# Counting the uncertain rows of a sparsemax on TensorE, with the flags of eight heads in one word

## The reference

```python
def sparsemax(x):                      # last axis: 722 scores
    x = x - jnp.max(x, axis=-1, keepdims=True)
    zs = -jnp.sort(-x, axis=-1)
    cssv = jnp.cumsum(zs, axis=-1) - 1.0
    support = zs > cssv / rho          # rho = 1, 2, ..., 722
    k = jnp.maximum(jnp.sum(support, axis=-1, keepdims=True), 1)
    tau = jnp.take_along_axis(cssv, k - 1, axis=-1) / k
    return jnp.clip(x - tau, 0.0)
scores = jnp.einsum('bhqd,bhkd->bhqk', qh, kh) * scale
out = jnp.einsum('bhqk,bhkd->bhqd', sparsemax(scores), vh)
```

## Time and profile before

| | |
|---|---|
| median of the three runs | 724.58 us |
| time of the profiled execution | 725.45 us |
| its span, first to last instruction | 723.7 us |
| PE busy | 584.8 us (81%) |
| DVE busy | 609.3 us (84%) |
| ACT, POOL busy | 380.7 us (53%), 187.1 us (26%) |
| mean granted TensorE clock | 0.902 of 2.4 GHz |

### The profile page before, as it was taken

The page is one execution under the profiler, slowest core; times in us unless marked ns, Lnnn a source line. Parts: engine busy times, 40 slices in busy tenths (PEclk is TensorE's granted clock), DMA queues, the critical chain, the costliest instruction groups (busy, mean ns, idle before and its releaser), DMA issues.

```text
span 723.7 us, 14347 instructions
## 1 busy us (share of the span) xinstructions
PE 584.8 (81%) x4560; PEld 332.5 (46%) x4560; DVE 609.3 (84%) x2964; ACT 380.7 (53%) x657; POOL 187.1 (26%) x239
## 2 busy tenths in 40 slices
PE   3785989798814998899899998990889988997575
PEld 1343545454402654565455544550445544655242
DVE  5699799977966999999999999994899999999600
ACT  3664565766611755666566646560456665563321
POOL 2511403241220240415033502351014430301301
PEclk9879978999965999999999999996899999996857
DMA  9752131202220113130303030303102111200000
GB/s 315 237 166 72 27 103 47 59 0 71 68 76 0 28 28 101 33 84 15 110 26 95 6 105 28 106 1 84 42 1 78 39 45 31 59 17 14 11 1 11
DMA packets 33471, 44.23 MB, mean 61 GB/s; under 512 B 8353, under 2 KB 26785, under 8 KB 33382
## 3 DMA queue, kind: packets, MB, share of 16 engines
q1 hardware_dynamic: 32332, 41.16, 20.0%
q10 hardware_dynamic: 1056, 2.10, 0.8%
HBM read 23.77 MB, written 1.64 MB: 35 GB/s over the span
## 4 chain that ended last, share of the span: by engine, by line
PE 64%; issue 16%; ACT 11%; DVE 4%; SPq 3%; DMA 1%; POOL 1%; POOLq 0%; DVEq 0%
PE ring L456 33%; PE ring L522 8%; PE ring L545 5%; PE ring L599 5%; PE mix_bank L570 5%; PE ring L495 4%; PE ring L507 3%; ACT qst L674 2%; ACT S L674 2%; SPq L248 2%; ACT ctx L674 1%; DMA S<-in_L_xattn_Wk 1%; SPq L252 1%; ACT v L674 1%; ACT ks L682 1%
## 5 line engine op out<-in xcount | busy, mean ns | idle before, releaser
L929 DVE MAX8 cand<-S 100x8 f32<-100x45 f32 (+1 forms) x2048 | 223.1, 188 | 0.5 <-issue 0.4
L456 PE MATMUL ring<-wv,ctx 128*121 128x512 f16 x576 | 156.7, 392 | 0.0
L456 PE MATMUL ring<-ctx,wk 128*128 128x361 f16 x768 | 136.1, 339 | 4.5 <-DVE ctx L1108 4.5
L798 ACT ACTIVATE pT<-ring 121x800 f32<-121x800 f32 x96 | 80.5, 839 | 75.2 <-PE ring L599 75.2
L674 ACT ACTIVATE S<-ring 100x722 f32<-100x722 f32 x128 | 95.2, 774 | 27.6 <-PE ring L545 27.2
L456 PEld LDWEIGHTS ring<-ctx,wk 128*128 128x128 f16 x768 | 78.9, 104 | 58.6 <-issue 14.9
L333 POOL TENSOR_TENSOR ctx<-ctx_f,ctx 128x484 f16<-128x484 f32 x42 | 50.6, 1205 | 163.8 <-ACT ctx L674 163.4
L545 PE MATMUL ring<-kst,qst 96*100 96x361 f16 x256 | 68.0, 361 | 29.4 <-ACT S L674 12.9
L456 PEld LDWEIGHTS ring<-wv,ctx 128*121 128x121 f16 x576 | 71.8, 137 | 33.4 <-issue 7.9
L599 PEld LDWEIGHTS ring<-qst,kst 99*121 99x121 f16 x768 | 61.5, 150 | 45.5 <-issue 21.7
L341 POOL TENSOR_TENSOR ks<-k_f,ks 128x361 f16<-128x361 f32 x64 | 57.2, 894 | 90.9 <-ACT k_f L686 88.2
(11 more groups left out here) (126 smaller groups left out, 727.3 us busy)
## 6 DMA issues: line engine op xcount, KB each, us to landing
kst<-ks SPq DMA_DIRECT2D x384, 45.1 KB, 1.9
ctx_f<-in_ctx SPq DMA_DIRECT2D x45, 242.0 KB, 2.9
xq<-in_x SPq DMA_DIRECT2D x8, 200.0 KB
xr<-in_x SPq DMA_DIRECT2D x8, 200.0 KB
out_y<-att SPq DMA_DIRECT2D x8, 200.0 KB
S<-in_L_xattn_Wk ACTq DMA_DIRECT2D x1, 1024.0 KB, 6.8
wq<-in_L_xattn_Wq ACTq DMA_DIRECT2D x1, 1024.0 KB, 11.3
wcos<-in_L_ffn_theta SPq DMA_DIRECT2D x1, 1024.0 KB, 10.4
```

The source lines that it names most:

```text
L456: last = nc.tensor.matmul(psum, lhs(c, i), w(c, j), start=(c == 0 and n == 0), stop=(c == DC - 1 and n == 2))
L798: nc.scalar.activation(pT[0:CK, u % 3, :, :], src, ACT.Relu).then_inc(two_read, 1)
L929: last = nc.vector.max(cand[:, h, 8 * n:8 * n + 8], S[0:L, HH * (i % 2) + h, cuts[n]:cuts[n + 1]])
```

## The change

Four things change.

1. The last Newton step takes its step at zero or more, and is written apart.
2. The test on DVE is one comparison: all eight ranks at or over tau, written as bf16 marks laid out by rank (`by_rank`: 8 ranks x 8 heads x 16 pieces; the comparison runs through `cand` in its own order, so successive marks go to places 128 marks apart). The first MAX8 of the next half waits for it.
3. PE does the sum: one product of `n_over`, then one of 128 columns for each rank, with minus ones for ranks 0 to 6 and ones for rank 7. It leaves 16 + 1 numbers a head in one PSUM row. `sum_flags(i)` moves from phase i + 1 to the end of phase i, right behind the scores of half i + 1 and ahead of `o_of` and the next keys.
4. `read_flags` sums the 17 numbers, multiplies each flag by 2^h, and sums them to one word. `settle` loads that word once, and tests fours, twos and ones of its bits by register arithmetic. Heads are refined from the lowest number up.

```diff
             def sum_flags(i):
                 pe.wait_ge(flag_ready, i + 1)
                 if i > 0:
                     pe.wait_ge(aT_ready, 2 * i)
-                nc.tensor.matmul(flag_ps, ones[:, :], n_over[:, :], start=True, stop=False)
-                nc.tensor.matmul(flag_ps, minus[:, :], n_now[:, :], start=False, stop=True).then_inc(flag_sum, 1)
+                nc.tensor.matmul(flag_ps[:, :, PIECES], ones[:, :], n_over[:, :], start=True, stop=True)
+                for r in range(8):
+                    last = nc.tensor.matmul(flag_ps[:, :, 0:PIECES], (one_b if r == 7 else minus_b)[:, :],
+                                            by_rank[:, r, :, :], start=(r == 0), stop=(r == 7))
+                last.then_inc(flag_sum, 1)
...
             def maxes(i, h):
                 dve.wait_ge(two_read, seen2(("s", i, h)))
+                if h == 0 and i > 0:
+                    dve.wait_ge(flag_ready, i)
...
-                    last = nc.vector.scalar_tensor_tensor(t, step_t[:, :], STRETCH[turn], t, ALU.mult, ALU.add)
...
+                nc.vector.scalar_tensor_tensor(t, step_t[:, :], 0.0, t, ALU.max, ALU.add).then_inc(tau_ready, 1)
                 dve.wait_ge(tau_ready, i + 1)
-                marks = over[:, :, :].rearrange("p g (n r) -> p g n r", r=8)
-                counted(nc.vector.tensor_tensor(marks[:, :, :, 7:8], pieces[:, :, :, 7:8],
-                                                t4.broadcast_to([L, HH, PIECES, 1]), ALU.is_lt))
-                n = counted(nc.vector.tensor_tensor(marks[:, :, :, 0:7], pieces[:, :, :, 0:7],
-                                                    t4.broadcast_to([L, HH, PIECES, 7]), ALU.is_ge))
-                n = counted(nc.vector.tensor_tensor(fold[:, :, 2:2 + NCAND // 2], over[:, :, 0:NCAND // 2],
-                                                    over[:, :, NCAND // 2:NCAND], ALU.add))
-                n = counted(nc.vector.reduce_sum(n_now[:, :], fold[:, :, :], AX))
-                nc.vector.scalar_tensor_tensor(n_now[:, :], n_now[:, :], -float(PIECES), n_over[:, :],
-                                               ALU.add, ALU.min).then_inc(flag_ready, 1)
+                nc.vector.tensor_tensor(by_rank.rearrange("p r g n -> p g n r"), pieces, t4.broadcast_to([L, HH, PIECES, 8]), ALU.is_ge).then_inc(flag_ready, 1)
...
+            def read_flags(i):
                 dve.sem_clear(check_step)
                 dve.wait_ge(flag_sum, i + 1)
-                nc.vector.scalar_tensor_tensor(code[:, :], flag_ps, 0.5, order_c[:, :],
+                nc.vector.reduce_sum(lost[:, :], flag_ps, AX).then_inc(check_step, 1)
+                dve.wait_ge(check_step, 1)
+                nc.vector.scalar_tensor_tensor(code[:, :], lost[:, :], 0.5, bit_c[:, :],
                                                ALU.is_gt, ALU.mult).then_inc(check_step, 1)
-                nc.vector.max(ranked[:, :], code[:, :]).then_inc(check_step, 1)
                 dve.wait_ge(check_step, 2)
-                nc.vector.tensor_copy(ranked_i[:, :], ranked[:, :]).then_inc(check_step, 1)
+                    nc.vector.reduce_sum(word_i[:, :], code[:, :], AX).then_inc(check_step, 1)
...
-                with dve.If(first > 0):
+                with dve.If(word > 0):
                     dve.wait_ge(tau_split, i + 1)
-                    with dve.Fori(0, HH // 2) as pair:
-                        leading = dve.value_load(ranked_i[0:1, bass.ds(2 * pair, 1)], min_val=0, max_val=HH)
-                        with dve.If(leading > 0):
-                            with dve.Fori(0, 2) as k:
-                                number = dve.value_load(ranked_i[0:1, bass.ds(2 * pair + k, 1)], min_val=0, max_val=HH)
-                                with dve.If(number > 0):
-                                    refine(i, number)
+                    with dve.Fori(0, 2) as four:
+                        with dve.If(((word >> (4 * four)) & 15) > 0):
+                            with dve.Fori(0, 2) as pair:
+                                with dve.If(((word >> (4 * four + 2 * pair)) & 3) > 0):
+                                    with dve.Fori(0, 2) as k:
+                                        with dve.If(((word >> (4 * four + 2 * pair + k)) & 1) > 0):
+                                            refine(i, 4 * four + 2 * pair + k)
                     split_again(i)
```

More of the change, by code:

```diff
@@ L1012, in test_sums, with refine @@
                 dve.wait_ge(fix, 3 + P // 32)
[L1014 to L1018 removed]
+            def refine(i, h):
+                h = nc.s_assert_within(h, 0, HH - 1, skip_runtime_bounds_check_because="a sum of three bits")
+                t = tau[:, i % 2, bass.ds(h, 1)]
+                row = S[0:L, bass.ds(h + HH * (i % 2), 1), :].rearrange("p a n -> p (a n)")
                 dve.sem_clear(fix)
@@ L1052, in rank_flags @@
                                                ALU.is_gt, ALU.mult).then_inc(check_step, 1)
-                dve.wait_ge(check_step, 1)
-                nc.vector.max(ranked[:, :], code[:, :]).then_inc(check_step, 1)
                 dve.wait_ge(check_step, 2)
-                nc.vector.tensor_copy(ranked_i[:, :], ranked[:, :]).then_inc(check_step, 1)
+                with nc.allow_low_precision(reason="a sum of distinct powers of two under 256"):
+                    nc.vector.reduce_sum(word_i[:, :], code[:, :], AX).then_inc(check_step, 1)
```

47 lines of the change are left out of this document (21 added, 26 removed).

## The result

The changed kernel takes 752.4 us (median of 4 runs, 750.8 to 753.1) beside 724.4 for the kernel before on the same chip: ratio 1.0383, 95% interval 1.0355 to 1.0410. The forecast was 733.0 with 717.5 to 743. The sign was right, the size was not: 28 us instead of 8.5.

The account below looks back on a forecast made before the run. The chain stands still at two refinements of flagged heads; elsewhere PE sets the pace. Terms +4.8 +0.8 +1.3 +1.7 +6.9 -7.0 = +8.5 us give 734.0 on the profiled execution, 733 as median, range 717.5 to 743.

Parts of the forecast that it names:

- PE's own part: PE's nine products take 0.55 us, +0.4 for each half; over the halves on the path, +4.8 us.
- The comparison: DVE's new instruction writing 1024 scattered marks takes 4.2 us; this was said to decide the sign.
- the bounds: DVE's new comparison lies between 1.22 us, as if written side by side, and 4.75 us at 4.5 ns a mark.
- The step that derived 3.9 ns a mark: DVE's two old comparisons take 1.65 us, leaving 0.5 for 128 marks; times 1024 plus 0.16 gives 4.15 us.
- Its reason, that a new place costs: In DVE's comparison, each access to a new 16-byte line is penalised, and every one of 1024 marks pays it.
- Where the loss falls on DVE: DVE's slower comparison adds +0.8 us before half 3, +1.3 before half 10 and +1.7 in the last half.
- The argument that DVE has time to spare: DVE waits 1.17 us for ACT in phase 7, so about 1 us to spare in 75; ordinary-half savings move nothing.
- The new wait of PE: At the earlier sum PE waits 2.1 us in phase 4, 1.6 in phases 8, 12 and 6, none in odd: +6.9.
- rival (c): Comparison at 4.75 us, longer waits: +17 us, 741, plus up to 1.1 us clock loss each; chance 0.50 together with forecast.
- The arrival in odd phases: In odd phases some 4.1 us lie between DVE's last tau and PE reaching the sum, so no wait.
- Settling: At flagged halves 3 and 10, removed list loads save 2.8 and 4.2 us on DVE: -7.0, between -3 and -10.
- the sign that it would be wrong about the loads: DVE's idle time round the refinements, forecast to fall from 18 us to about 11, stays over 15.

Follow-up runs that it names:

- run 8: Kernel before with eight further products of 128 columns, of constants, behind its two at the old place: 727.1 us, ratio 1.0011.
- run 4: Probe on the changed kernel: marks side by side, seven separate comparisons in place of one, three with unused results; 795.6 us, one run, a time that means nothing.
- run 2: Changed kernel with the sum put back at its old place, slow comparison kept: 735.9 us, ratio 1.0173.
- run 7: Changed kernel with four-byte marks by rank and the sum at its old place: 725.3 us, ratio 0.9971.
- run 11: Changed kernel, comparison of 4.72 us kept, with only its odd phases' sums back at the old place: 745.1 us, ratio 1.0283.
- run 13: Kernel before with the word of bits tested by fours, twos and ones in place of the ranked list: 720.4 us, ratio 0.9928.
- run 14: Changed kernel with the ranked list and its loads in place of the word of bits: 756.7 us, ratio 1.0428.
- run 12: Two variants of the changed kernel: one loop of eight single bit tests, or the innermost test made twice; one run each, read for gaps, no total time given.
- run 15: Kernel before with lost heads counted beside their ranked list and one loop running just that many times: 713.9 us, ratio 0.9833.
- run 5: Changed kernel with four-byte marks by rank, PE reading the upper two bytes, sum at the new place: 734.1 us, ratio 1.0118.
- run 6: Changed kernel with the comparison walking by rank, reading apart and writing two-byte marks side by side, sum at the new place: 734.7 us, ratio 1.0128.
- run 9: Changed kernel with four-byte marks, only the even phases summing at the new place, odd ones at the old: 727.0 us, ratio 1.0014.

## Why the prediction was wrong

By ratios, from the kernel before to the changed one: the word of bits -5 us; the sum of four-byte marks by PE at the old place, with the new last step of tau and the wait of the first MAX8, +3 (0.9971 less 0.9928; no run parts these); their comparison made the dear one, +15 (1.0173 less 0.9971); the place, +15. In the other order the place comes to 10.7 and the comparison to 19, so each makes the other dearer. The intervals leave some 3 us on each. The profiled spans of the same kernels, 719.9, 723.2, 731.5 and 750.9, put the third step at 8 and the fourth at 19.

**PE's own part: about right.** Nine products take 0.62 us at full clock, forecast 0.55; an even phase grew by 0.6 us, forecast 0.4, and 0.46 of that is the products alone (run 8).

**The comparison: right in kind, low in size.** 4.2 was taken, 4.72 came, inside the bounds; all 1024 marks pay as L969's do. The step that derived 3.9 ns a mark from the pair of old comparisons underrated it by 0.5 us (4.5 ns came). Its reason, that a new place costs, was only half of it: two-byte marks are what is dear (run 4).

**Where the loss falls on DVE: failed.** The prediction let it act before halves 3 and 10 and in the last half, for 3.8 us. At the old place the dear comparison cost 8 to 15. In the profiles of runs 2 and 7 it shows as PE's waits ahead of attend: 1.88 and 1.86 us at halves 4 and 8, where the cheap comparison has none, and 6.43 for 3.06 at half 14, 7.1 us of the spans' 8.3. None of these halves was in the forecast. The argument that DVE has time to spare, by its wait for ACT, was read in phase 7 and carried to all.

**The new wait of PE: the step that failed.** It had +6.9 us, made of 2.1 and three times 1.6 in even phases and none in odd ones, and it took the wait itself as the whole price. The waits came to 6.5 us, but in other places (3.67 in phase 4, 2.8 in odd phases), and the price is not in them: the five odd phases 5 to 13, put at nothing but PE's own part, grew by 14.4 us, of which 1.8 are waits and 3.0 the nine products (five times 0.6). The other 9.6 us (an estimate by this difference) go with the lower clock of the same rows: mean clocks of 0.92 and 0.88 for 0.96, and 0.86 for 0.90 in phase 11. Across kernels with the same nine products, the odd phases 5, 7, 9 and 13 lasted 38.5 to 38.7 us at 1.00, 39.6 to 41.1 at 0.96, 41.1 to 42.3 at 0.92 and 43.1 to 43.4 at 0.88. The prediction priced the clock, at up to 1.1 us per wait, only inside rival (c) and only for even phases.

The places failed for a second reason. The arrival in odd phases was right (28.0 us behind attend, 28.2 before), but 4.72 us do not fit into 4.1, so they wait; rival (c), at that very length, should have had these waits and left them out. With the odd phases lengthened, DVE, which is not slower there, gains on PE: the comparison of half 6 starts at 334.51 us and PE comes at 340.28, 5.8 us apart where the earlier trace rows had 2.9. That removes the forecast waits. Put the odd sums back, which leaves the odd phases at 40.3 us, and the waits appear (run 11), 2.0 to 2.3 us each. So the prediction priced each wait at fixed spacing, while a phase that grows changes the spacing of the next. Phase 4, which follows a settling, grew by 5.5 us instead of some 2.5: 3.67 of it is the wait, behind a comparison of 5.47 us.

**Settling: right in sign, too large, for the wrong reason.** -7.0 was forecast, -3 to -5 measured. The idle time was to fall from 18 us to 11 and stayed at 17.8, which the prediction had named as the sign that it would be wrong about the loads; like for like, the word took 2.5 to 2.7 us from it (runs 13 and 14). A passing test is nearly free, a failed one costs about 1.2 us with its jump and turn (run 12), and a loop without failed tests saved 11.5 us (run 15). There were as many failed tests on the new way as on the old, or nearly: in half 10 three instead of four. By the floor of 600 ns for a register load that the Trainium skill gives (DMA: Bandwidth & Descriptors, Latency and other measured facts) twelve loads would give back 7.2 us as an estimate; those 2.5 to 2.7 us went. Its 51 and 108 ns for branches (Advanced Engine Details and Errata, Control Flow Timing) do not come near the 1.2 us of a failed test with its jump.

What stays open: what makes the clock stay low behind the scores of an odd phase. The place of the sum bears on the time, but both kernels of runs 5 and 6 show the low clock without a wait, run 7 shows it in phase 5 at the old place, and run 9 had it in phase 7 (0.96) and not in phase 9 (1.00) with the same code. Nor do the profiles bear out that the wait lengthens it: in those of the four kernels with the dear comparison at the new place (the changed one, both of run 12, run 14), the seven phases among 5, 7, 9 and 13 without a wait all have 0.88 and last 43.1 to 43.3 us, and the nine with a wait of 0.5 to 0.8 us have 0.92 or 0.96 and last 41.1 to 42.3. Which of the two brings about the other is not shown. Nor does a run tell why the comparison of phase 4 takes 5.47 us instead of 4.72.

## What to carry to other kernels

Cost a layout on both of its sides: a step that is free for the engine that writes may be four times as slow for the one that reads, and the form between them (wide marks read in half, or a walk in the reader's order) can serve both. Where two engines run nearly level, a phase that one of them takes longer over moves the meeting points of the following ones, so forecast the sequence of phases, not a sum of single waits. On data-dependent control flow, count the tests that fail, and let a loop's bound do the skipping.

## What the runs showed of the hardware

DVE writes two-byte results apart at 4.6 ns each (4.72 us for 1024), four-byte ones at 1.9 (1.94 us), and two-byte ones side by side at 1.2 (1.22 us). 128 single ones, 128 pairs and 128 fours take 0.73 to 0.74 us. PE reads two-byte operands at a step of 4 bytes as fast as side by side (223 and 226 ns for a product from start to end), and at 16 bytes in 405 ns, at either clock. A test on DVE that fails costs about 1.2 us over a long body, by six of them in run 12; a second one that passes moved one gap from 3.87 to 3.89 us, and the two others got shorter. The same code had gaps that differ by up to 2.9 us between builds (2.02 and 4.94). The granted clock can give back most of what added products take: eight more in each half, 0.46 us of work each time, cost 0.8 us in all (-1.0 to 2.6).
